# Two attention layers around a mixture of experts: rows normalised three batches ahead, loads and sums four ahead, the sixth weight subtraction on GpSimd

## The reference, cut to what matters

```
x = x + tanh(g0) * xattn0(layernorm(x), ctx, mask0)        # 16 heads of 16, 77 keys, output projection
x = x + tanh(g1) * moe(layernorm(x))                       # 8 experts, top 2 of 8, gelu gate, F = 1024
x = x + tanh(g2) * xattn1(layernorm(x), ctx, ctx, mask1)   # the same attention with biases
x = x + tanh(g3) * fourier(layernorm(x))                   # fft, sparse complex weight, real ifft, bias
```

## Time and profile before

| | |
|---|---|
| median of three runs | 1344.51 us (1343.1 to 1349.46) |
| the profiled execution: its own time | 1344.64 us |
| its span, first to last instruction | 1343.1 us |
| mean granted TensorE clock | 0.931 of full speed |
| busy share TensorE, VectorE, ScalarE, GpSimd | 84%, 65%, 44%, 21% |
| chain that ended last, by engine | PE 63%, DVE 11%, ACT 9%, issue 7%, DMA 5%, POOL 2% |

### The profile page before, as it was taken

The page is one execution under the profiler, slowest core; times in us unless marked ns, Lnnn a source line. Parts: engine busy times, 40 slices in busy tenths (PEclk is TensorE's granted clock), DMA queues, the critical chain, the costliest instruction groups (busy, mean ns, idle before and its releaser), DMA issues.

```text
span 1343.1 us, 32603 instructions
## 1 busy us (share of the span) xinstructions
PE 1124.6 (84%) x10697; PEld 944.7 (70%) x10698; DVE 868.1 (65%) x2583; ACT 593.2 (44%) x1251; POOL 280.7 (21%) x383
## 2 busy tenths in 40 slices
PE   5178778787778999999999999999996778878886
PEld 3166667666657878788887878888874666666664
DVE  4057766767856666575766767675565577777773
ACT  3156655556624242332424242332233565666663
POOL 6302433433342000000000000000013233344410
PEclk9588988889878999999999999999997899999998
DMA  8754555545538513131220313100024344444430
GB/s 253 238 136 124 158 150 142 149 129 153 170 136 280 210 45 106 42 101 47 70 89 32 116 40 119 40 29 29 25 86 123 99 113 121 119 122 113 121 82 25
DMA packets 143662, 150.55 MB, mean 112 GB/s; under 512 B 41418, under 2 KB 111280, under 8 KB 141433
## 3 DMA queue, kind: packets, MB, share of 16 engines
q1 hardware_dynamic: 122982, 82.97, 22.9%
q0 software_dynamic: 14960, 57.44, 12.8%
q10 hardware_dynamic: 5616, 8.78, 1.8%
HBM read 80.80 MB, written 58.84 MB: 104 GB/s over the span
## 4 chain that ended last, share of the span: by engine, by line
PE 63%; DVE 11%; ACT 9%; issue 7%; DMA 5%; POOL 2%; ACTq 2%; SPq 1%; DVEq 0%; another core or an unknown queue 0%; POOLq 0%
PE bank L1978 25%; PE bank L1991 13%; PE bank L1797 6%; PE bank L1664 4%; PE bank L1644 3%; DVE bm L1279 3%; ACT h L966 2%; ACT pr L1005 2%; PE bank L1732 2%; PE bank L1740 2%; ACT pr L1004 2%; DMA query_halves<-qT 2%; PE bank L1808 1%; DVE pr L525 1%; ACT hT L957 1%
## 5 line engine op out<-in xcount | busy, mean ns | idle before, releaser
L1978 PE MATMUL bank<-tiles,we 128*128 128x256 f16 (+1 forms) x3744 | 393.7, 259 | 5.8 <-issue 4.9
L1978 PEld LDWEIGHTS bank<-tiles,we 128*128 128x128 f16 x3744 | 325.3, 98 | 46.4 <-issue 13.4
L1143 ACT ACTIVATE tiles<-bank 128x256 f32<-128x256 f32 (+1 forms) x312 | 109.3, 353 | 333.5 <-PE bank L1978 302.9
L1991 PE MATMUL bank<-we,tiles 128*128 128x256 f16 x1608 | 224.1, 274 | 16.2 <-DVE tiles L1576 15.5
L1572 DVE SCALAR_TENSOR_TENSOR tiles<-bank,tiles 128x256 f32<-128x256 f32 (+1 forms) x312 | 119.9, 384 | 158.3 <-ACT tiles L1143 153.7
L1991 PEld LDWEIGHTS bank<-we,tiles 128*128 128x128 f16 x1608 | 147.8, 98 | 53.5 <-DVE tiles L1576 29.1
L1004 ACT ACTIVATE pr<-bank 116x512 f32<-116x512 f32 x192 | 108.9, 567 | 103.3 <-PE bank L1740 99.4
L1279 DVE TENSOR_REDUCE bm<-bank 128x6 bf16<-128x462 f32 (+1 forms) x192 | 105.2, 578 | 61.1 <-PE bank L1708 59.9
L1578 DVE TENSOR_TENSOR tiles<-tiles 128x256 f16<-128x256 f32 (+1 forms) x312 | 121.1, 388 | 11.1 <-DVE tiles L1576 0.5
L525 DVE TENSOR_TENSOR pr<-pr 116x512 f16<-116x512 f32 x160 | 109.1, 683 | 25.6 <-ACT pr L1005 23.0
L1732 PE MATMUL bank<-qop,kop 125*116 125x256 f16 (+1 forms) x352 | 98.8, 303 | 18.2 <-ACT pr L1005 16.2
(11 more groups left out here) (204 smaller groups left out, 1697.9 us busy)
## 6 DMA issues: line engine op xcount, KB each, us to landing
qop<-query_halves SPq DMA_DIRECT2D x96, 144.0 KB, 3.2
wes<-in_guT POOLq DMA_DIRECT2D x9, 1024.0 KB, 5.1
query_halves<-qT SPq DMA_DIRECT2D x32, 256.0 KB
expert_out<-zeros POOLq DMA_DIRECT2D x4, 2048.0 KB, 17.9
tiles<-expert_in SPq DMA_DIRECT2D x29, 256.0 KB, 2.7
pr<-in_guT POOLq DMA_DIRECT2D x7, 1024.0 KB
yg<-in_dnT POOLq DMA_DIRECT2D x7, 1024.0 KB, 6.4
expert_out<-tiles ACTq DMA_DIRECT2D x28, 256.0 KB, 2.1
```

The source lines that it names most:

```text
L1978: last = pe.matmul(bank[1 + fc % 3][:, half * S:half * S + w * P], gate_up[:, par, c, i, col:col + P], xT[:, j, c, 0:w * P], start=n == 0, ...
L1991: last = pe.matmul(bank[4 + t][:, 0:D], act16[:, fc % 4, i, t * P:(t + 1) * P], we[:, par, 2, j, fc * D:(fc + 1) * D], start=fc == 0 and n ...
```

## The change

`steps` now keeps 2 to 11 in the loop and ends `ld` after b = 11. The batch b+3 (where there is one: `third`) is measured, rooted, scaled and normalised in step b, loads and, in layer 1, gathers and sums are for b+4. With `POOL_LOW = (5,)` the sixth subtraction is GpSimd's, behind its gathers. ScalarE and TensorE take h_hi, q_hi, t_h and proj_q earlier in the step. In layer 1 the sum is stored to DRAM (`x2_scratch`), and the base is loaded from there. At the start of layer 0, late masks, late weights (`load_late`) and Fourier tables (`load_fourier`) are issued later, the padding of the keys takes 3 DMAs a layer, not 8, and the count of late masks (`counts(8, ..)`) goes into the first step. The removed lines of the old order that stand again elsewhere are partly cut.

```diff
-POOL_LOW = ()
+POOL_LOW = (5,)
...
     step(at(layer, 1), True, True, True, True)
-    step(at(layer, 2), True, True, True, True)
     with eng.Fori(0, 5) as j:
+        step(Batch(layer, j * 2 + 2, j + 1, 0), True, True, True, True)
         step(Batch(layer, j * 2 + 3, j + 1, 1), True, True, True, True)
-        step(Batch(layer, j * 2 + 4, j + 2, 0), True, True, True, True)
+    step(at(layer, 12), True, True, True, False)
     step(at(layer, 13), True, True, True, False)
     step(at(layer, 14), True, True, False, False)
     step(at(layer, 15), False, True, False, False)
+def third(b):
+    return not (isinstance(b.i, int) and b.i > NB - 4)
...
+def pad_keys(layer):
+    pads = keys_d[layer, :, :, H:].rearrange("d i h n -> (d i) (h n)")
+    n = (HEADS - H) * KEYS
+    for first in range(0, n, 2 * D * QT):
+        end = min(n, first + 2 * D * QT)
+        sp.dma_start(pads[:, first:end],
+                     zeros[0:2 * DH].rearrange("p t n -> p (t n)").bitcast(F16)[:, 0:end - first]
+                     ).then_inc(s.keys_padded, 16)
+pad_keys(0)
+for par in range(2):
+    sp.dma_start(vbd[:, par].rearrange("p j i n d -> p (j i n d)"),
+                 a["vones"]).then_inc(s.spread_tables_in, 16)
+load_weights(3, s.attention_weights_in)
...
+def load_late():
+    sp.dma_start(raw_one, a["mask1T"]).then_inc(s.layer_mask_in, 16)
+    sp.dma_start(raw_late, a["mask0T"][:, 4 * S:]).then_inc(s.late_masks_in, 16)
+    for k in range(NW // 2, NW):
+        load_weights(k, s.late_weights_in)
...
-    if isinstance(b.i, int) and b.i < 2:
-        if b.layer == 1:
-            sp.wait_ge(s.combine_step, b.i * 3 + 3)
     if not (isinstance(b.n, int) and b.n < 2):
         sp.wait_ge(s.row_update, b.n - 1)
-    src = rows(x_d, b.i * S) if b.layer == 0 else xin[:, b.par]
+    if b.layer:
+        sp.wait_ge(s_sum[b.par], 16 * (b.own + 1))
+    src = rows((x_d, x2_d)[b.layer], b.i * S)
     sp.dma_start(xb[:, b.par], src).then_inc(s_base[b.par], 16)
+def store_sum(b):
+    sp.wait_ge(s.combine_step, b.i * 3 + 3)
+    sp.dma_start(rows(x2_d, b.i * S), xin[:, b.par]).then_inc(s_sum[b.par], 16)
...
-        if not tail:
-            sp.wait_ge(s.normed, 2)
-        load(b.after(3))
+        sp.wait_ge(s.normed, b.n + 3)
+        load(b.after(4))
...
+    if isinstance(b.i, int) and b.i == 1:
+        load_fourier()
+        pad_keys(1)
+        sp.wait_ge(s.mask_flags, 5)
...
-base(at(0, 0))
 for m in range(KC):
     sp.wait_ge(s.bulk_low, (1, 2)[m])
     store_keys(0, m, 0)
-sp.wait_ge(s.queries_padded, 288)
+sp.wait_ge(s.normed, 1)
+load(at(0, 2))
+sp.wait_ge(s.mask_flags, 1)
+load_masks(at(0, 0))
+load_masks(at(0, 1))
+sp.wait_ge(s.queries_padded, 32)
+sp.wait_ge(s.keys_padded, 48)
 sp.wait_ge(s.keys_stored, 32 * KC)
 load_keys(at(0, 0), 0)
-sp.wait_ge(s.mask_flags, 1)
-load_masks(at(0, 0))
 store_queries(at(0, 0))
 load_queries(at(0, 0))
-load_keys(at(0, 1), 0)
-load_masks(at(0, 1))
 load_second_queries(at(0, 0))
 load_keys(at(0, 0), 1)
-sp.wait_ge(s.normed, 1)
-load(at(0, 2))
+load_keys(at(0, 1), 0)
+load_keys(at(0, 1), 1)
 store_queries(at(0, 1))
-load_keys(at(0, 1), 1)
 load_queries(at(0, 1))
 load_second_queries(at(0, 1))
+sp.wait_ge(s.normed, 2)
+load(at(0, 3))
+base(at(0, 0))
 for block in range(1, 3):
     for m in range(KC):
         sp.wait_ge(s.bulk_low, (4, 5, 9, 10)[2 * block - 2 + m])
         store_keys(0, m, block)
 load_maxima(at(0, 0))
 sp.wait_ge(s.keys_stored, 32 * 3 * KC)
-sp.wait_ge(s.mask_flags, 5)
+load_late()
...
+    if third(b):
+        store_sum(b.after(3))
+    if ld:
+        sp.wait_ge(s.normed, b.n + 3)
+        sp.wait_ge(s_sum[b.par], 16 * (b.after(2).own + 1))
+        load(b.after(4))
     if not (isinstance(b.i, int) and b.i < 2):
         store(b.after(-2))
     if front:
         base(b.after(1))
     if pre:
         operands(b.after(2))
-    if ld:
-        if not tail:
-            sp.wait_ge(s.normed, NB + 2)
-        sp.wait_ge(s_base[(b.par + 1) % 2], 16 * (b.after(1).half + 1))
-        load(b.after(3))
-    if pre:
         load_keys(b.after(2), 1)
...
     if part:
-        wait_apart(pool, s.places_recalled, b.i + 4)
-    if part:
-        gather(b.after(3), 0)
-    if pre:
-        root(b.after(2))
-    if part:
-        gather(b.after(3), 1)
-        gather(b.after(3), 2)
+        wait_apart(pool, s.places_recalled, b.i + 5)
+        gather(b.after(4), 0)
+        gather(b.after(4), 1)
     if tail:
         ln_root(1, s.root_after, s.variance_after, pv)
+    if third(b):
+        root(b.after(3))
     if part:
-        gather(b.after(3), 3)
+        gather(b.after(4), 2)
+        gather(b.after(4), 3)
+    w_low(b, G - 1)
...
+pool.wait_ge(s.pool_setup, 5)
+root(at(0, 0))
+root(at(0, 1))
 pool.dma_start(gates[:], a["gates"].partition_broadcast(P)).then_inc(s.small_inputs_in, 16)
 for k, name in enumerate(BIASES):
     pool.dma_start(brow32[:, k], a[name].rearrange("(o d) -> o d", o=1)).then_inc(
         s.small_inputs_in, 16)
 pool.dma_start(wg[:], a["gwT"].rearrange("(c p) e -> p c e", p=P)).then_inc(s.small_inputs_in, 16)
-pool.wait_ge(s.pool_setup, 5)
-root(at(0, 0))
-root(at(0, 1))
+root(at(0, 2))
...
 gather_whole(at(1, 1))
+root(at(1, 1))
 gather_whole(at(1, 2))
-root(at(1, 1))
+root(at(1, 2))
+gather_whole(at(1, 3))
...
-    for g in range(1, 5):
-        expo(b, g)
+    expo(b, 1)
     if pre:
-        h_norm(b.after(2))
         h_hi(b.after(2))
+    expo(b, 2)
+    expo(b, 3)
+    if pre:
+        q_hi(b.after(2))
+    expo(b, 4)
+    if tail:
+        h2_norm(pv)
+    if front:
+        v_spread(nx, 0)
     expo(b, 5)
     if tail:
-        h2_norm(pv)
-    if pre:
-        q_hi(b.after(2))
-    if tail:
         tail_out(pv)
+    if third(b):
+        h_norm(b.after(3))
     if front:
-        v_spread(nx, 0)
+        v_spread(nx, 1)
         m_out(nx)
...
     w_low(b, 0)
-    if pre:
-        pre_stats(b.after(2))
     w_low(b, 1)
     if tail:
         residual(pv)
     w_low(b, 2)
     if tail:
         update_stats(pv)
+    if b.layer == 0 and not (isinstance(b.i, int) and b.i < 2):
+        place(b.after(-2))
+    w_low(b, 3)
     if pre:
-        pre_norm(b.after(2))
-    w_low(b, 3)
+        q_low(b.after(2))
+    if tail:
+        renorm(pv)
     if front:
         maxima(nx, 0)
         maxima(nx, 1)
-    if tail:
-        renorm(pv)
-    if b.layer == 0 and not (isinstance(b.i, int) and b.i < 2):
-        place(b.after(-2))
+    if third(b):
+        pre_stats(b.after(3))
     w_low(b, 4)
     if front:
         maxima(nx, 2)
         maxima(nx, 3)
-    if pre:
-        q_low(b.after(2))
-    w_low(b, 5)
+    if third(b):
+        pre_norm(b.after(3))
     if front:
         maxima(nx, 4)
         maxima(nx, 5)
+    w_low(b, 5)
     if ld and b.layer == 1:
-        recall(b.after(4))
-        combine(b.after(3))
+        recall(b.after(5))
+        combine(b.after(4))
...
+recall(at(1, 3))
+combine(at(1, 2))
+pre_stats(at(1, 2))
 for g in range(GP):
     maxima(at(1, 0), g)
-combine(at(1, 2))
-recall(at(1, 3))
+pre_norm(at(1, 2))
+recall(at(1, 4))
+combine(at(1, 3))
...
     scores(b, 0)
+    pe.wait_ge(s.values_spread, 2 * b.n + 2)
     scores(b, 1)
-    pe.wait_ge(s.values_spread, 2 * b.n + 2)
     if tail:
         t_att(pv)
     scores(b, 2)
...
         if b.layer == 0 and isinstance(b.i, int) and b.i == 1:
             pe.wait_ge(s.bias_rows_in, 16)
         proj_o(pv)
+    if pre:
+        t_h(up2)
     values(b, 0)
     scores(b, 3)
     values(b, 1)
-    scores(b, 4)
-    if front:
-        top_scores(nx, 0)
-        top_scores(nx, 1)
-    values(b, 2)
-    scores(b, 5)
-    if pre:
-        t_h(up2)
-    if front:
-        top_scores(nx, 2)
-    values(b, 3)
     if pre:
         pe.wait_ge(s.normed_high, up2.n + 1)
     if ranked:
...
         else:
             pe.wait_ge(s.queries_low, nx.n + 1)
         proj_q(up2)
+    scores(b, 4)
+    values(b, 2)
+    if b.layer == 0 and isinstance(b.i, int) and b.i == 1:
+        pe.wait_ge(s.unmasked_rows, 2)
     if front:
-        top_scores(nx, 3)
+        top_scores(nx, 0)
+        top_scores(nx, 1)
     if ranked:
         pe.wait_ge(s.ranks_read, b.i - 1)
+    if front:
+        spread(nx, 0)
+    scores(b, 5)
+    values(b, 3)
+    if front:
+        top_scores(nx, 2)
+        top_scores(nx, 3)
+        pe.wait_ge(s.values_spread, 2 * nx.n + 1)
     if tail:
         t_h2(pv)
+    values(b, 4)
     if front:
         top_scores(nx, 4)
-    values(b, 4)
-    if front:
         top_scores(nx, 5)
     if tail:
         pe.wait_ge(s.normed_after_high, pv.n + 1)
     if front:
-        spread(nx, 0)
+        spread(nx, 1)
         t_mask(nx)
-        pe.wait_ge(s.values_spread, 2 * nx.n + 1)
-        spread(nx, 1)
     values(b, 5)
     if tail:
         if pre:
...
             logits(pv)
         else:
             token_major(h2T, mf, B_FOURIER, s.fourier_out)
+    if b.layer == 0 and isinstance(b.i, int) and b.i == 0:
+        pe.wait_ge(s.mask_flags, 5)
```

(2 more changed lines are left out.)

64 lines of the change are left out of this document (31 added, 33 removed).

## The result

The changed kernel takes **1397.91 us** (median of four, 1396.3 to 1398.27), the kernel before beside it 1343.8 (1341.89 to 1349.46): ratio 1.039, interval 1.036 to 1.043. The profiled execution took 1398.13 us with a span of 1396.6.

What follows compares the result with a forecast made beforehand. No engine is full, so the order of waits in the two attention stages bounds the kernel. From 1344.6 us: -11.5 + 7 + 5 + 32 - 2 = +30.5, giving 1375 us; range 1302 to 1396.

Steps and rivals of the forecast that it cites:

- What is taken away: Attention steps: TensorE's wait for normalised rows h, 51.2 us in all, goes; the gain if nothing else is late.
- rival (a): Attention steps: the h wait goes and nothing replaces it, GpSimd's subtraction ending in time; 1287 us, chance 0.15.
- A step of layer 1: Gathering steps of layer 1: next step starts at 20.5 instead of 17.6, +2.9 in 11 steps, +32 us.
- the ring: Layer 1: closed chain of scores, projection, statistics, root, gathers, subtraction, values, scores; +2.9 us in every gathering step.
- until here nothing is worse by more than 1.4 us: Layer-1 step up to pre_stats at 12.35: VectorE's delays, third subtraction at 6.9 not 5.54, stay within 1.4 us.
- A step of layer 0: Layer-0 steps: the h wait is exchanged for a VectorE that is never idle; +0.5 in 14 steps, +7 us.
- I let what the low stretches cost stand as it is: Both attention stages: low-clock cost taken as unchanged, mean granted clock 0.87 and 0.94; change priced on undisturbed steps.
- The start of layer 0: First steps: 30 us won on the first maxima, but GpSimd and queued transfers delay the second step; -11.5 us.
- GpSimd's gate: Start of layer 0: root 3 and first sixth subtraction, behind late masks, flags and clearing, done at 79.
- the collision: Start of layer 0: 6 MB just issued delay the second step's maxima and bias rows; 2 us (0 to 8).
- The start of layer 1: First layer-1 steps: roots ahead of gathers delay VectorE's first subtraction from 1038.38 to 1045; partly hidden, +5 us.
- the last steps: Last four layer-1 steps, without gathers: h wait gone and VectorE loses 0.41; -2 us for them all.

Runs made afterwards that it cites:

- e12: Rows normalised one step ahead and the new start kept, all engines' step order as before, all subtractions on VectorE; 1288.61 us, ratio 0.965 to the kernel before.
- e3: Changed kernel with all four gathers of a layer-1 step at the head of GpSimd's step, ahead of both roots; 1384.54 us, ratio 1.028.
- e2: Changed kernel with all six subtractions on VectorE, the sixth behind the last maxima; 1400.09 us, ratio 1.039.
- e1: Changed kernel with GpSimd's sixth subtraction moved ahead of the second pair of gathers; 1402.35 us, ratio 1.040.
- the put-back runs: e12 with one part of the changed kernel's order put back at a time; e14 took 1356.11 us, e13 1322.81.
- e5: e3 with ScalarE's copy h_hi moved behind the third pair of exponentials; 1380.59 us, ratio 1.028.
- e6: e3 with 22 matmuls of zeros a step added where TensorE waits for VectorE; 1403.52 us, ratio 1.044.
- e9: e6 with 8 float32 matmuls of zeros a step in place of 22; 1391.55 us, ratio 1.036.
- e14: e12 with TensorE's and ScalarE's whole step order of the changed kernel put back; 1356.11 us, ratio 1.015.
- e13: e12 with VectorE's late statistics of the batch three ahead put back, root behind root_after on GpSimd; 1322.81 us, ratio 0.990.
- e10: Changed kernel with GpSimd's first weight fetch and eight clearing transfers issued behind its first step, not ahead; 1395.1 us, ratio 1.038.

## Why the prediction was wrong, step by step

**What is taken away: right, and worth more than I let it be.** The wait went from 51.2 to 7.6, and where nothing new was late (e12 against before) the steps of layer 0 fell by 30.2 us, the gathering ones of layer 1 by 24.5 (e12's chip runs the kernel before 0.7% faster than the traced one). That is rival (a), which I gave 0.15, true of the idea and not of this kernel. That its 1287 and e12's 1288.61 are so close is partly luck: (a) counts 11.5 won at the start, and e12's first residual comes 1.9 later than before.

**A step of layer 1: right sum, wrong mechanism.** The walk met the trace within 0.3 us at each point up to the start of the subtraction, and +32 met +31.8. The second is luck: the terms, which add up to 20.4 and not 20.5, gave a step of 20.5 for 17.6, the measured means are 21.4 for 18.5. The failed step is the ring itself. I named GpSimd's queue as what closes it, and all rings through that queue hold 11 of the 32 (e3; e2 10, e1 none). I took from the last values to the next scores the 2.11 of before, at full clock; the output product there takes 1.91 for 1.03 a half, 20.4 us in the layer, more than all rings through GpSimd. And I passed over the rest with the remark "until here nothing is worse by more than 1.4 us". In the put-back runs TensorE's and ScalarE's order costs 27.7 us over these 11 periods and the late statistics 8.6. The 1.4 itself, the third subtraction behind the early copy, is not what does it: on e3, e5 took it away and won 0.7 us in these periods. The price of the subtraction, 1.08, was 0.66; I had in VectorE's 0.41 and twice that a better one at hand.

**A step of layer 0: the sign right, the size mis-sized, +16.7 for +7.** The failed step is "I let what the low stretches cost stand as it is". The reordering makes gaps ahead of the maxima, the granted clock falls from 0.87 to 0.76 in that stage, and logits, first scores, the turn and half of the output projection then run at 1.2 GHz, the lower of the two levels; the 1.1 us a step that layer 0 lost lie just there. The low clock is not a cause by itself, though: with the gaps filled (e6, e9) layer 0 took 305.3 and 285.0, where e3 took 278.2, for waits without a named releaser came in its place. The order of the queues is what moves it: e12 to e14 is +32.2, to e13 +23.8. My sign that VectorE would be over 80% busy was wrong, it was at 69% (137.57 of 200): it waits, 89.1 us in all, for ScalarE's exponentials.

**The start of layer 0: -1.8 for -11.5.** GpSimd's gate was right within 3 us. The failed term is the collision, 2 us, which came to 7.6 (3.35 and 4.24), near its upper bound of 8; the first scores, forecast near 43, came at 45.69, and the second step at 83.97 for 80. e10 shows that the two do not add: 7 us taken from the queue gave 2.9.

**The start of layer 1 and the last steps:** +5.4 for +5; +1.2 for -2, with the new order still in them (in e12 they take 3.2 less than before).

**The range** ended at 1396, too low mainly for want of the two terms that were mis-sized, +9.7 each (the last steps add 3.2). The rivals were all about what GpSimd does; none was about the order of TensorE's own instructions, though the diff is mostly that.

## What to carry to other kernels

Split a change into the idea (work one step ahead) and the new order of each queue, and price them apart: here the idea was worth -3.5% and two of the reorderings took more than twice that. In a pipeline with several nearly full engines a new order must be priced to the end of the step, also by the gaps that it leaves on TensorE: here the last product of a step paid for gaps that lay ahead of the maxima. A delay that is easy to see (the third subtraction behind the copy) needn't be the one that sets the step; take it away by itself before you name it. Filling the gaps brought the clock back and not the time. And where two engines stand for no reason that the profile names, look at when the signals that they wait for were sent.
